# Attention in a decoder layer: bfloat16 parts in one array against float32r parts in two row groups

## The reference, cut to what matters

```python
# self attention: q, k with rotary embedding, ALiBi bias on earlier keys, softmax over all 2048 keys
attn = einsum('bhqd,bhkd->bhqk', q, k) * SCALE
attn = attn + where(pos_k - pos_q > 0, 0, pos_k - pos_q) * slopes[h] * 8.0
out = einsum('bhqk,bhkd->bhqd', softmax(attn), v);  x = layernorm(x + out @ proj_w.T + proj_b)
# cross attention: q from x, k and v from the 1601 context rows, no bias
scores = einsum('bhqd,bhkd->bhqk', q, k) / sqrt(16);  x = layernorm(x + (softmax(scores) @ v) @ Wo.T)
# experts: router, best two of eight, two-layer perceptrons
x = layernorm(x + mixture(x))
```

## Time and profile before

| | us |
|---|---|
| median of 3 runs (lowest, highest) | 2590.88 (2575.44, 2608.23) |
| the profiled execution, its own time | 2585.78 |
| its span, first to last instruction | 2584.0 |
| start to the first max pass of self attention | 157.9 |
| self attention, first to last head's maximum (L1100) | 196.3 to 1027.3 |
| cross attention, the same | 1226.0 to 1883.6 |
| mean granted clock of TensorE | 0.91 |

### The profile page before, as it was taken

The page is one execution under the profiler, slowest core; times in us unless marked ns, Lnnn a source line. Parts: engine busy times, 40 slices in busy tenths (PEclk is TensorE's granted clock), DMA queues, the critical chain, the costliest instruction groups (busy, mean ns, idle before and its releaser), DMA issues.

```text
span 2584.0 us, 40898 instructions
## 1 busy us (share of the span) xinstructions
PE 2209.6 (86%) x12836; PEld 1102.0 (43%) x12836; DVE 1511.0 (58%) x3272; ACT 1250.5 (48%) x2408; POOL 374.7 (15%) x374
## 2 busy tenths in 40 slices
PE   7679999999999999855999999999985478888870
PEld 3434444444444444331333333333333366767660
DVE  5758777777777777156887878788825300000006
ACT  2205666666666667621676766666671022222110
POOL 0001111111111111100122212222220400000013
PEclk9869999999999999975999999999996589999885
DMA  7320100000010000002000000000000443434322
GB/s 233 98 77 1 34 31 24 22 22 23 28 34 26 22 22 1 6 1 82 12 13 24 13 23 15 19 19 13 12 1 3 160 159 135 152 134 151 135 84 83
DMA packets 94028, 138.63 MB, mean 54 GB/s; under 512 B 13193, under 2 KB 76338, under 8 KB 93284
## 3 DMA queue, kind: packets, MB, share of 16 engines
q1 hardware_dynamic: 90436, 127.13, 14.7%
q0 software_dynamic: 3360, 8.58, 1.1%
HBM read 102.97 MB, written 32.31 MB: 52 GB/s over the span
## 4 chain that ended last, share of the span: by engine, by line
PE 71%; DVE 9%; DMA 8%; SPq 4%; issue 3%; POOL 2%; ACT 2%; POOLq 0%; ACTq 0%; DVEq 0%
PE B L736 18%; PE B L724 12%; PE B L674 12%; PE B L883 7%; DMA XS<-xsD 5%; PE B L717 5%; PE B L692 4%; PE B L677 4%; DVE CM L1095 3%; PE B L796 2%; PE B L721 2%; PE B L681 2%; ACT PT L940 1%; POOL xsD L607 1%; PE B L628 1%
## 5 line engine op out<-in xcount | busy, mean ns | idle before, releaser
L1095 DVE TENSOR_REDUCE CM<-B 128x1 f32<-128x512 f32 (+1 forms) x2048 | 1175.5, 634 | 302.7 <-PE B L674 160.5
L940 ACT ACTIVATE PT<-B 128x512 f32<-128x512 f32 x1856 | 1010.8, 597 | 610.3 <-PE B L724 500.1
L674 PE MATMUL B<-oper 109*128 109x416 bf16 (+3 forms) x1600 | 529.4, 358 | 26.4 <-DMA oper<-kxD 24.3
L724 PE MATMUL B<-oper 112*128 112x512 bf16 (+3 forms) x1408 | 513.4, 371 | 13.3 <-issue 9.2
L736 PE MATMUL B<-PT,VS 128*32 128x512 f32 x3712 | 497.7, 608 | 3.9 <-ACT PT L940 1.9
L566 POOL TENSOR_TENSOR OH<-wrot,one 128x512 fp32r<-128x512 f32 x128 | 133.0, 1039 | 1518.1 <-ACT wrot L931 1518.1
L724 PEld LDWEIGHTS B<-oper 112*128 112x128 bf16 x1408 | 134.4, 97 | 334.3 <-ACT PT L940 240.4
L1250 DVE COPY YS<-B 128x256 f32<-128x256 f32 x46 | 19.5, 425 | 439.6 <-PE B L883 439.6
L674 PEld LDWEIGHTS B<-oper 109*128 109x128 bf16 x1600 | 157.6, 99 | 265.5 <-DVE CM L1095 177.7
L677 PE MATMUL B<-oper 109*128 109x512 bf16 (+3 forms) x640 | 222.9, 361 | 15.4 <-DMA SD<-sdD 13.3
L717 PE MATMUL B<-oper 112*128 112x512 bf16 (+3 forms) x640 | 224.2, 353 | 7.4 <-issue 6.1
(11 more groups left out here) (168 smaller groups left out, 1488.9 us busy)
## 6 DMA issues: line engine op xcount, KB each, us to landing
W<-in_w1T_dram SPq DMA_DIRECT2D x23, 1024.0 KB, 7.1
W<-in_w2T_dram SPq DMA_DIRECT2D x23, 1024.0 KB, 5.8
oper<-kD SPq DMA_DIRECT2D x32, 192.0 KB
xsD<-YG SPq DMA_DIRECT2D x1, 5888.0 KB, 19.9
XS<-xsD SPq DMA_DIRECT2D x23, 256.0 KB, 6.9
ysD<-YS SPq DMA_DIRECT2D x23, 256.0 KB, 6.0
oper<-kD SPq DMA_DIRECT2D x32, 128.0 KB
qD<-parts SPq DMA_DIRECT2D x8, 384.0 KB, 2.5
```

Of the source, the lines that this page charges most:

```text
L674: mm = pe.matmul(slot[:, 0:low], q, KO[0:A_ROWS, c2, 0, k0:k0 + low], start=True, stop=True, skip_group_check=True)
L724: mm = pe.matmul(bank[:, up:QB], stat[0], QO[0:B_ROWS, c, q0 + up:q0 + QB], start=(up == 0), stop=True, skip_group_check=True)
L940: act.activation(PT[:, (c * plan.nu + u) % PRING, :], S[(c * plan.nu + u) % SBANKS][:, :], ACT.Exp).then_inc(A.exps, 1)
L1095: dve.tensor_reduce(CM[:, a, b:b + 1], slot[:, 0:ch], AX.X, ALU.max).then_inc(A.freed, 1)
```

## The change

- q and k are split into two float32r parts, and 3 products of them are taken: 48 rows, 4 bias rows and 2 shift rows, 54 in all. Queries 0 to 1023 stand in the array's rows 0 to 63, queries 1024 to 2047 in rows 64 to 127 (`QO` has both halves, `KO` is loaded twice); items and units alternate between the two row groups.
- The max pass takes 32 items of 1024 keys (2 x 402 keys an item in cross attention) instead of 64 chunks. An item is two matmuls into two neighbouring PSUM banks; the ring has 2 slots of two banks. The two matmuls of an item are issued as two beats, ahead of successive score units. The max pass has no bias rows in effect: VectorE adds the bias from a table (`tensor_tensor_reduce`: add, then maximum, and a bfloat16 output that nobody reads), in 24 of the 32 items; GpSimd makes the table of each head in 8 pieces.
- Key tiles are outside in the score pass: batch b is key tile b with 4 query blocks, and the output of all 4 blocks accumulates in one bank (`OA`). There is one save, one sums item (four transposes) and one division per head. `pv_batch` runs behind the third unit of a batch.
- All key tiles use the biased key matrix; GpSimd sets the bias rows of a query tile to zero when the key tile has passed it (`A.zeroed`). The query bias rows are therefore loaded anew for each head, in `place_shift`: 8 DMAs in self and 4 in cross attention instead of 3.
- At the start, VectorE no longer makes `SD` for all heads (GpSimd makes it per head), GpSimd adds the projection's bias to x, and SyncE issues the loads of the first three heads ahead of the stores of the cross keys.

```diff
...
+HL = 2
+BIAS_ROWS = 4
+PAIR_ROWS = 3 * D
+M_ROWS = BIAS_ROWS + PAIR_ROWS
+S_ROWS = M_ROWS + HL
+HALF = N // 2
+SUM_AT = 2
 LEAD = 3
 RING = 3
 PRING = 12
...
+RSLOTS = 2
+TABLE = N - P + HALF
+XCH = 402
...
+    def fills(self, first, end, ahead):
+
+
+        return [("max", n // 4 + TT // 2 * (n % 2), n // 2 % 2, ahead) for n in range(first, end)]
+
+    def order(self, b):
+
+
+        return (2, 3, 0, 1) if self.first((b + LEAD) % self.nb) % 2 == 0 else (0, 1, 2, 3)
...
         if b == self.nb - LEAD + 1 and not (whole and h + 1 >= H):
-            items.insert(2, ("shift", 0, 0, 1))
+            items.append(("shift", 0, 0, 1))
+        if b == SUM_AT and not (whole and h == 0):
...
+        R = [banks[:, (SBANKS + 2 * i) * QB:(SBANKS + 2 * i + 2) * QB] for i in range(RSLOTS)]
+        OA = B[7]
...
+                        sp.dma_start(q[0:2 * D, :], qsrc[0:2, head, cols]).then_inc(ld, 16)
+                        sp.dma_start(q[2 * D:3 * D, :], qsrc[0, head, cols]).then_inc(ld, 16)
+                        sp.dma_start(k[0:2 * D, :], ksrc[0:1, head, :].to_broadcast([2, D, plan.nk * P])).then_inc(ld, 16)
+                        sp.dma_start(k[2 * D:3 * D, :], ksrc[1, head, :]).then_inc(ld, 16)
+                        if alibi:
+                            sp.dma_start(KF32[64 * g + 1:64 * g + BIAS_ROWS:2, c, :],
+                                         slD[bass.ds(h * 6, 6), :][0:4:2, :]).then_inc(ld, 16)
...
                 def place_shift(h, c):
                     sp.wait_ge(A.freed, plan.shift_end(h))
-                    for s in range(PARTS):
-                        sp.dma_start(QO[A_ROWS + s:A_ROWS + s + 1, c, :],
-                                     MT[s * TT:(s + 1) * TT, :]).then_inc(A.shift_loaded, 16)
-
+                    for g in range(2):
+                        cols = slice(g * HALF, (g + 1) * HALF)
+                        if alibi:
+                            q = QF32[64 * g:64 * g + BIAS_ROWS, c, :]
+                            sp.dma_start(q[0:BIAS_ROWS:2, :], slD[bass.ds(h * 6, 6), cols][0:4:2, :]).then_inc(A.shift_loaded, 16)
+                            sp.dma_start(q[1:BIAS_ROWS:2, :], negD[:, cols].to_broadcast([2, HALF])).then_inc(A.shift_loaded, 16)
+                        for s in range(HL):
+                            t0 = s * TT + g * TT // 2
+                            sp.dma_start(QF32[64 * g + M_ROWS + s:64 * g + M_ROWS + s + 1, c, :],
+                                         MT[t0:t0 + TT // 2, :].bitcast(F32)).then_inc(A.shift_loaded, 16)
...
+                if alibi:
+                    store_parts(PREP1[16:], 16)
                 place_shift(0, 0)
 
...
+                    if alibi:
+                        for s in range(3):
+                            pool.tensor_tensor(SD[:, c, s, :], idb[:, :], slPF[:, s, bass.ds(h, 1)].to_broadcast([P, P]), ALU.mult)
                     pool.tensor_copy(VS[:, c, 0:nk, 0:D], V[:, 0:nk, bass.ds(h * D, D)]).then_inc(A.v, 1)
...
+                    lo, hi = cuts[piece], cuts[piece + 1]
+                    dst = table0 if isinstance(h, int) and h == 0 else tables[c]
+                    pool.tensor_tensor(dst[:, lo:hi], base[:, lo:hi], sl8[:, bass.ds(h, 1)].to_broadcast([P, hi - lo]),
+                                       ALU.mult).then_inc(A.table, 1)
...
+                        else:
+                            at = 4 * (kt - 1) + plan.order(kt - 1).index(kt // 4)
+                            pool.wait_ge(A.scores, plan.nu * h + (at + 1))
+                        pool.sem_inc(s_cue, 1)
+                        g, col = kt // 8, kt % 8 * P
+                        pool.tensor_copy(QO[64 * g:64 * g + BIAS_ROWS, c, col:col + P], zeros[64 * g:64 * g + BIAS_ROWS, :]).then_inc(A.zeroed, 1)
+                        pool.wait_ge(A.zeroed, TT * h + (kt + 1))
...
+                        elif ahead and 3 <= kt <= 10:
+                            pool.sem_inc(s_cue, 1)
+                            table(h + 2, (c + 2) % RING, kt - 3)
...
+                    pool.wait_ge(s_vs, TT + NXP // P)
+                    for i in range(3):
+                        pool.wait_ge(s_st[i], 16 * (NPREP // 3))
+                    for h in range(1, RING):
+                        stage(h, h)
+                        for piece in range(8):
+                            table(h, h, piece)
...
+                        g = a // (TT // 2)
+                        col = a % (TT // 2) * P
+                        for n in range(2):
+                            k0 = (2 * b + n) * ch
+                            mm = pe.matmul(slot[:, n * QB:n * QB + ch], QO[64 * g:64 * g + M_ROWS, c2, col:col + P],
+                                           KO[64 * g:64 * g + M_ROWS, c2, k0:k0 + ch], start=True, stop=True)
+                            if n == 0:
+                                yield
...
+                        pe.transpose(slot[:, 0:P], SHW[:, :], idf[:, :]).then_inc(A.filled, 1)
...
+                        pe.wait_ge(A.saved, h + (1 + ahead))
                         for t in range(4):
-                            for part in (OH, OL):
-                                mm = pe.matmul(slot[:, t * 32:t * 32 + D + 2], part[:, a % 2, t * P:(t + 1) * P], selR[:, :],
-                                               start=(part is OH), stop=(part is OL), skip_group_check=True)
+                            mm = pe.transpose(slot[:, t * P:(t + 1) * P], OS[:, t * P:(t + 1) * P], idf[:, :])
                         mm.then_inc(A.filled, 1)
...
+                    u = 4 * b + n
+                    kt, qb = b, plan.order(b)[n]
...
+                    diag = alibi and kt // 4 == qb
+                    if diag:
+                        pe.wait_ge(A.zeroed, TT * h + (kt + 1))
...
+                    g, q0 = qb // 2, qb % 2 * QB
+                    mm = pe.matmul(bank, KO[64 * g:64 * g + S_ROWS, c, kt * P:(kt + 1) * P],
+                                   QO[64 * g:64 * g + S_ROWS, c, q0:q0 + QB], start=True, stop=not diag, skip_group_check=True)
...
+                        lo = kt % 4 * P
+                        for s in range(3):
+                            mm = pe.matmul(bank[:, lo:lo + P], SD[:, c, s, :], dTS[:, :],
+                                           start=False, stop=(s == 2), skip_group_check=True)
...
+                    if b == 0 and not (isinstance(h, int) and h == 0):
+                        pe.wait_ge(A.saved, h)
+                    for n in range(4):
+                        qb = plan.order(b)[n]
...
-                            ring(items[cuts[n]:cuts[n + 1]])
-                            if n == 1 and b > 0:
+                            for beat in beats[cuts[n]:cuts[n + 1]]:
+                                next(beat)
+                            scores_unit(b, n, h, c)
+                            if n == 2 and b > 0:
...
+                def save(h):
+
+                    act.wait_ge(A.pv, plan.nb * (h + 1))
+                    if not (isinstance(h, int) and h == 0):
+                        act.wait_ge(A.freed, plan.ring_before(h + 1))
+                    act.activation(OS[:, :], OA, ACT.Copy).then_inc(A.saved, 1)
...
+                    x0 = b * HALF - a * P
...
+                        dve.wait_ge(A.table, 8 * h + 8 * (1 + ahead))
+                    dve.wait_ge(A.filled, pos + 1)
...
+                            dve.tensor_reduce(CM[:, a, b:b + 1], slot.rearrange("p (n k) -> p n k", n=2)[:, :, 0:ch],
+                                              AX.XY, ALU.max).then_inc(A.freed, 1)
+                        elif not biased:
+                            dve.tensor_reduce(CM[:, a, b:b + 1], slot, AX.X, ALU.max).then_inc(A.freed, 1)
+                        else:
+                            src = table0 if isinstance(h, int) and h + ahead == 0 else tables[(c + ahead) % RING]
+                            at = x0 + N - P
+                            dve.tensor_tensor_reduce(skip[bank % 2], slot, src[:, at:at + HALF], 1.0, -3.0e38,
+                                                     ALU.add, ALU.max, CM[:, a, b:b + 1]).then_inc(A.freed, 1)
+                        if (a, b) == (TT - 1, 1):
...
```

More of the change, by code:

```diff
@@ L70, with __init__, first @@
 class Plan:
[L74 removed]
+    def __init__(self, nk, chunk):
         self.nk = nk
[L76 to L77 removed]
+        self.chunk = chunk
         self.nu = NQB * nk
[L79 to L88 removed]
+        self.nb = nk
+        self.nm = 2 * TT
+        self.prologue = self.fills(0, self.nm, 1) + [("shift", 0, 0, 1)] + self.fills(0, self.first(LEAD), 2)
+    def first(self, slot):
+        return self.nm * slot // self.nb
+    def fills(self, first, end, ahead):
+        return [("max", n // 4 + TT // 2 * (n % 2), n // 2 % 2, ahead) for n in range(first, end)]
+    def order(self, b):
+        return (2, 3, 0, 1) if self.first((b + LEAD) % self.nb) % 2 == 0 else (0, 1, 2, 3)
     def ring_items(self, b, h):
@@ L93, in ring_items @@
         items = []
-        for q in range(NQB):
```

(19 more changed lines are left out.)

536 lines of the change are left out of this document (230 added, 306 removed).

## The result

The changed kernel takes 2786.93 us (median of 4 runs, 2783.84 to 2800.86) against 2598.66 us before: ratio 1.075, 95% interval 1.066 to 1.084. It is slower, and above the highest time of my range, 2740. The profiled execution took 2784.33 us.

What follows compares the result with a forecast made beforehand. TensorE's streaming was taken to bound attention before, the two-slot ring in self attention after. 2585.8 + 54 (self heads) - 5 (cross attention) - 26 (start) + 1 (prologue) - 4 (tails) = 2606 us; range 2495 to 2740.

Steps and rivals of the forecast that it cites:

- the start: Before the first max pass: loads go out at about 84 us, first max pass at 132, -26 us (bounds -34 and -15).
- cross attention: Same chain through batches of two and three items: 42.7 us a head against 43.0, -5 us in all.
- the half clock: Behind TensorE's wait at each self head's start: slower clock adds 1.0 us a head (bounds 0 and 1.7).
- the length of the chain: Self attention's ring of two slots: closed TensorE-VectorE chain, 3.2 us a batch, 51.2 a head, plus 0.10 per biased item.
- changed parity and sums item: Self head: slots change parity at shift and sums items, 0.9 us twice; the sums item itself some 0.8.
- wait for the shift: Self head's start: eight DMA issues land 6.3 us behind the copy, TensorE waits 3.8, adding 2.8 us a head.
- prologue of the max pass: Max pass before the first head: 36.5 us against 38.4, plus the biased items' extra, +1 us.
- Streaming on TensorE: Attention batches: float32r matmul 0.218 us, row groups overlap with 0.11 between starts; TensorE needs 2.3 us a batch against 3.4.
- Loop turn: Where the loop over heads turns: 58.6 instead of 54.8 us at three heads goes into the shift's wait.
- Rival 4: Same chain, unseen terms at high ends: heads of 62.5 (self) and 44.4 us (cross), 2680 us; chance 0.15.
- rival 1: Unseen costs all at low ends: chain 3.0 us, heads 52.6 and 40.7 us, total 2475 us; chance 0.22.
- Rival 3: TensorE: float32r streams 512 columns in 0.43 us; total 2790 us with overlap, 3190 without; chance 0.09.

Runs made afterwards that it cites:

- e10_warm: Changed kernel with 18 useless matmuls on TensorE ahead of the shift wait at each self head but the first: 2780.65 us, ratio 1.069.
- e5_same_group: Changed kernel with query block order turned round, so unit and preceding max-pass beat share a row group: 2997.48 us, ratio 1.152.
- e1: Changed kernel with self attention's multiplication by v behind the second unit instead of the third: 2688.0 us, ratio 1.036.
- e4: Changed kernel without the bias in the maximum, all items plain reductions: 2748.81 us, ratio 1.059.
- e2_lead4: Changed kernel with LEAD 4 instead of 3, so max pass and shift come one batch earlier: 2750.73 us, no ratio.
- e6_merge: Changed kernel with four shift DMAs instead of eight in self attention, two instead of four in cross attention: 2721.98 us, ratio 1.052.
- e8: Changed kernel with edits of e1, e6_merge, e2_lead4, cross-key stores before loads, and earlier multiplication in cross attention's two-item batches: 2538.78 us, ratio 0.980.

## Why the prediction was wrong, step by step

The mechanisms in the heads were the right ones, but their terms were too small; the terms of the start and of cross attention had the wrong sign. The steps that failed are the half clock (1.0 us a self head against 3.3), the length of the chain (2.8 us a head too short), the start (26 us gained against 13.7 lost) and cross attention (5 us gained against 31 lost). The forecast was 2606, 181 us under the measured median.

| term | forecast us | measured us |
|---|---|---|
| chain, 16 turns with the biased item | 52.8 | 55.5 (16 x 3.47) |
| changed parity and sums item | 2.6 | 2.8 (0.94 in one batch; 0.38, 0.37, 1.10 in e10_warm) |
| wait for the shift | 2.8 | 3.3 (6.76 - 3.47, e10_warm) |
| half clock behind it | 1.0 | 3.3 (65.0 - 61.7) |
| a self head | 59.2 | 65.0 |
| a cross head | 42.7 | 44.2 |
| first max pass | at 132 | at 171.6 |
| prologue of the max pass | 39.4 | 43.7 |

- **Streaming on TensorE.** The rate was near (0.218 taken, 0.24 in e5_same_group) and the overlap was right. The stagger of 0.11 us holds only for the first pair of a batch (0.09, behind the wait for VectorE); the other pairs start together. TensorE's own batch was put at 2.3 us; with the chain open it is 2.69 (e1). This miss cost nothing here, since the chain is longer. Two links of the chain were too short. From the first beat to the multiplication by v it is 0.51 us and not 0.42, though the uncovered weight load of 0.10 ahead of the first beat, which I had added, does not show (0.05 from VectorE's end to the beat). And the second beat's way to VectorE was taken from a bfloat16 matmul: 0.42 us; it is 0.54 for a plain item (e4). The beat is the first behind the multiplication. That an uncovered weight load adds the 0.12 there is argued, not shown.
- **The ring of two slots** was the right chain, by the run that opens it (3.47 to 2.69). It was sized 3.2 and 0.1, and measured 3.47: 2.8 us a head, of which the biased item's 0.16 instead of 0.10 is 1.0.
- **The shift.** 5.45 us of issues (4.3 to 5.8) and 6.9 us from copy to TensorE (6.3, bounds 5.5 to 7.0) were within the bounds. e2_lead4, which removes the wait, and e6_merge, which halves the issues, confirm the step.
- **Half clock.** This term failed most per head: 1.0 with bounds 0 and 1.7, measured 3.3. I took an idle time of 2.0 us as the model; here it is 4.1, and everything behind it is slow, VectorE's wait for the beats too. The upper bound was not a bound: it came from one case with a shorter wait. And the clock falls in places without a wait as well (e2_lead4, e10_warm), for a reason that no run shows.
- **Loop turn.** It does go into the same wait: the three heads at the turns take 63.9 to 65.0 us and do not stand out.
- **Start.** Wrong in sign: the first max pass came 13.7 us later than before, where I had it 26 earlier. The loads go out at 95.8 us and not at 84, and I counted their 30 issues at 0.6 us, 18 us; they took 39, as several queue for 2.3 to 3.0 us each while earlier loads are still moving. I also saw that the stores stood behind them and TensorE's projections behind the stores, and still put the first max pass at 132. Undoing the order gives 140.1.
- **Prologue.** +1 forecast, 5.3 in fact (43.7 against 38.4). The granted clock is 0.53 there, where it was 0.63 before; how much of the 5.3 is the clock's no run shows.
- **Cross attention.** -5 forecast, +31 measured: the shift's wait is 0.9 a head (e6), the chain binds in the two-item batches (e8), and the first head and two at the loop's turns take 51.0, 53.9 and 51.4 us (before 40.8 for the first and 47.3 to 49.4 at the turns). In each of the three the clock is 0.50 for 20 us or more.
- **The rest.** 14 us in the experts, at lower clock, with unchanged code. In the other runs this part took from 698 to 740 us, so it is scatter that no step could have given.
- **Range.** Rival 4 (2680, all high ends) had the right terms, but it too held the start's gain and the half clock at 1.7; the sum for rival 1 comes out at 2472 and not 2475. Rival 3 gives nearly the measured time, 2790, by a mechanism that the runs exclude.

Put back together, against the profiled execution's 2784.3: 15 x 5.8 = 87 us in the self heads, less 10 since the first and the last heads are shorter; 44 up to the first maxima (19 measured against -26 + 1); 36 in cross attention; 3.5 between, 14 behind, and 4 in tails that I had credited. The sum is 178. This is the account of one execution, with the clock's drops away from the waits in it as they fell.

## What to carry to other kernels

With a ring of two slots, ask for each item what TensorE issues between opening and closing it, and let nothing long stand there; an odd item belongs in the middle of a batch, since at the end it gives the next batch the slot that was filled last. Halving an engine's work pays only when the waits around it are shortened with it: the same matmuls took 2787 or 2530 us by the order alone. Cost an idle time of TensorE with the half clock behind it, here 3.3 us for 4.1 us of idle, and do not count on the full clock where the waits are short. Cost DMA issues in a long row from rows with the queue full.

## What the hardware showed unexpectedly

- Two float32r matmuls of 512 columns in different row groups start within the same 0.01 us (0.09 apart where TensorE had just waited for VectorE), and the next pair goes off 0.34 us later when the first pair followed an idle time or the multiplication; in an unbroken row within one group the distance is 0.24.
- An issue of two strided rows took 0.59 us, of four adjacent rows of one table 0.26 us, and of 16 partitions into two rows 0.67, the same as 8 partitions into one row (0.69).
- The clock can stay at its lower level for over 20 us: in e10_warm from 480 to 504, behind 2.44 us without work, though TensorE was busy for most of it. It can also fall where TensorE stood idle for no more than 0.80 us at a time in the 15 us in front: at 404.9 in the same run, for 20.5 us, and at 402.6 in e2_lead4, for 54.6 us.
